# A two-block graph network on one core: where three conversions, the exponentials and the lane comparisons stand in the window stage

## The chip, the cores and the metric

The kernel runs on one core of a Trainium2 chip. The metric is the device time of the core in microseconds, from launch to end; lower is better. The engines named below are PE (matmuls), DVE (VectorE), ACT (ScalarE), POOL (GpSimd) and SP (SyncE, which issues most transfers). Each engine works through its own queue in order, and waits in it on semaphores that the others raise.

## What is computed

Two blocks over 1250 nodes with 512 features and 20000 edges, sorted by destination:

```python
h = maximum(layernorm(x), 0)
# block 0
xn   = batchnorm(h)                              # over the nodes
agg  = segment_sum(xn[src], dst) / max(deg, 1)
conv = relu(agg @ W_conv + b_conv)
attn = performer_attention(h[0:256], Wq, Wk, Wv, Wo, proj)   # 8 heads, 256 features
x = x + batchnorm(conv + attn_rows + h)
h = maximum(layernorm(x), 0)
# block 1
agg = segment_sum(h[src], dst)
z = relu(batchnorm(((1 + eps) * h + agg) @ W1 + b1))
x = x + h + relu(batchnorm(z @ W2 + b2))
```

The features of attention are `exp(u - diag - max) / 16 + 1e-6`, with the maximum over a row for queries and over a whole head for keys. `attn_rows` gives each node the attention row of its place, with node 255's row for all nodes beyond the 256th.

## The kernel before

Both segment sums are done as matmuls with a matrix of edge counts `AT` (1250 x 1250, fp16), which the kernel builds itself. The nodes are cut into 25 windows of 50 destinations. For window t, DVE writes two one-hot matrices of the window's edges: `S` (the lane of the source, one comparison for 8 chunks of 125 edges, L893) and `ring` (a code of source tile and destination, one comparison for each chunk, L897, eight to a window). PE multiplies them chunk by chunk (8 matmuls, "the counts of window t") and raises `s_win`; ACT copies the result from its bank into `AT` (L547, `AT<-bank`). From window 8 on all counts use bank 0, so the counts of window t also need ACT's copy of window t-1.

Between the counts of two windows PE does the pieces of one step, listed in `SLOTS[t]`. Step t is: PE the pieces of `SLOTS[t]`, then the counts of window t. The names that matter here:

- `hT0` to `hT9`: transposes of the normalized rows; `K`, `Q`, `V`: projections; `FR` (step 4): the sum of squares of `W_conv`, from which ACT and POOL make one scale `wscale`; `P` (step 4): small transposes.
- Attention for a pair g of heads goes through `UKg`, `MXg` (maximum over a head), `QTg`, `KVg`, `UQg`, `Og`. ACT takes the exponentials of keys in piece `MXg` (L592, L593, then L598 for the scale) and those of queries in `UQg` (L609, L610). DVE gives the biases `nbk` and `nbq` for them (L922, L929). `MXg`, `KVg` and `Og` share bank 6, so that `MX1` waits until DVE has drained `O0` (L940).
- `Gi` (steps 8 to 17, one row tile of 125 nodes each): the normalized tile times `W_conv`, as 12 fp16 matmuls over 512 columns with high and low parts (`hn_hi`, `hn_lo`, `wC_hi`, `wC_lo`). Its input comes as follows: ACT applies the batch norm (`normed(i)`, L639, four instructions into `hn`, after POOL has the scales `bn_s`, `bn_t`), DVE splits it (`normed_parts(i)`: L984 `hn_hi`, L985 `hn_lo`, which frees `hn` again), and for the weights ACT writes `wC_hi` (L649, waits for POOL's `wscale`) and DVE `wC_lo` (L1123). `hn_hi` lies where `wC` lay, so the first split waits for `wC_lo`.
- `Ri`, one step after `Gi`: PE subtracts the fp16 copy `hh` of the result (ACT's `conv_high(i)`, L547 `hh<-bank`) in the bank, and ACT reads the rest as `hl` (`conv_low(i)`). R opens with a wait for `hh`.
- `D` and `A`: degrees and the aggregation with `AT`.

What sets the order is written out by hand. ACT goes through each step as: `normed(i+2)` for a G of the step before; the pieces of the step, sorted by `late` (0 for most, 1 for `UQ` and `MX`, 2 for G, so `hh` of a step comes behind its exponentials); `conv_weights_high()` at t = `SPLIT_AT` = 5; the copy of the counts of window t. DVE goes through step t as: `low_counts(t-1)` and `further_chunks(t)`, two branches for windows or edges out of the usual bounds, neither body of which is taken for this input; `first_chunks(t+1)`, which waits for `s_win`, then writes `S` and the eight `ring`; stats of transposed tiles; `wC_lo` at t = 6; `normed_parts(t-7)`; the pieces of the step. The first and second row tile are normed on ACT at t = 6 and 7 and split on DVE at t = 7 and 8.

## Time and profile before

| | us |
|---|---|
| device time, median of 3 runs | 400.58 (400.35 to 402.19) |
| the profiled execution: device time | 401.03 |
| the profiled execution: span from first to last instruction | 399.2 |
| PE busy in the span | 363.8 |
| DVE / ACT / POOL busy | 238.6 / 174.3 / 94.5 |

The device time of the profiled execution is 1.8 us above its span; times inside are us from the span's start. The window stage takes the stretch from about 16 to 171 us, the rest is the aggregation, the second norm and block 1. A row of the timeline names start, duration, engine, line, what is written and read, and in brackets how long the engine was idle before it and who ended that. Matmuls overlap, so the distance between two starts says what one costs, not its duration.

### The profile page before, as it was taken

How to read it: one execution, taken by the hardware profiler on the slowest of the kernel's cores; microseconds unless marked ns; L12 is line 12 of the kernel's file. 1: busy time of each engine (PE TensorE's matmuls, PEld its weight loads, DVE VectorE, ACT ScalarE, POOL GpSimd, SP SyncE). 2: the span in 40 equal slices, each digit the busy share in tenths (PEclk: the TensorE clock that was granted, in tenths of full speed). 3: DMA queues.
4: the chain of work that ended last, by engine and by line, in shares of the span. 5: the costliest groups of instructions: out<-in, count | busy, mean ns of one | idle time of the engine just before them, and what ended most of it. 6: DMA issues, size and time to landing. Idle time of an engine off the chain costs nothing.

```text
span 399.2 us, 6078 instructions
## 1 busy us (share of the span) xinstructions
PE 363.8 (91%) x2031; PEld 277.5 (70%) x2031; DVE 238.6 (60%) x642; ACT 174.3 (44%) x302; POOL 94.5 (24%) x147
## 2 busy tenths in 40 slices
PE   2799983997988899999998989899999999999994
PEld 1587643675766566767655656457999999999992
DVE  5878788676576388662897788611335445421324
ACT  1446556457556513612016769312355353333031
POOL 7110101000000000000013588932265744201100
PEclk9999998799899899999999999999999999999999
DMA  6990300000000000000590020300000003020212
GB/s 187 267 253 8 106 3 2 1 2 1 3 2 3 2 2 2 2 2 2 137 226 3 1 87 21 108 2 2 0 0 2 0 2 105 0 53 13 66 51 77
DMA packets 16584, 18.03 MB, mean 45 GB/s; under 512 B 1813, under 2 KB 10965, under 8 KB 16537
## 3 DMA queue, kind: packets, MB, share of 16 engines
q1 hardware_dynamic: 15779, 17.28, 16.1%
q8 instruction: 25, 0.41, 0.4%
q10 hardware_dynamic: 758, 0.16, 0.2%
q14 instruction: 22, 0.18, 0.2%
HBM read 14.88 MB, written 2.56 MB: 44 GB/s over the span
## 4 chain that ended last, share of the span: by engine, by line
PE 68%; DVE 13%; issue 8%; ACT 4%; POOL 3%; DVEq 2%; DMA 1%; SPq 1%; POOLq 0%; ACTq 0%
PE bank L1262 65%; DVE ring L897 2%; DMA x_in<-x 1%; DVE hl L1150 1%; POOL ln_s L456 1%; DVE w_lo L1169 1%; DVE st L975 1%; POOL x L492 1%; PE bank L1283 1%; DVEq L1019 1%; DVE st_row L1161 1%; DVE hn_lo L985 1%; PE bank L1629 1%; DVE x L1158 1%; ACT hh L739 1%
## 5 line engine op out<-in xcount | busy, mean ns | idle before, releaser
L1262 PE MATMUL bank<-AT,hh 125*128 125x400 f16 (+1 forms) x240 | 81.0, 339 | 2.6 <-DVE hl L1150 2.6
L1262 PE MATMUL bank<-AT,hl 125*128 125x400 f16 (+1 forms) x240 | 80.7, 338 | 0.5 <-issue 0.5
L465 POOL TENSOR_TENSOR bn_tmp<-var_eps,minus_half 128x1 f32<-128x1 f32 (+1 forms) x15 | 9.6, 643 | 202.1 <-DVE var_eps L991 202.0
L897 DVE TENSOR_SCALAR ring<-iota_code,code 125x250 f16<-125x250 f16 x200 | 46.0, 305 | 0.0
L1262 PEld LDWEIGHTS bank<-AT,hh 125*128 125x128 f16 x240 | 23.2, 97 | 21.6 <-DVE hl L1150 3.2
L1262 PEld LDWEIGHTS bank<-AT,hl 125*128 125x128 f16 x240 | 23.4, 97 | 18.7 <-issue 1.0
L893 DVE TENSOR_TENSOR S<-iota_lane,slo 125x1024 f16<-125x1024 f16 x25 | 18.7, 748 | 29.4 <-PE bank L1262 18.4
L1262 PE MATMUL bank<-a_hi,w_hi 128*128 128x400 f32 (+1 forms) x96 | 34.2, 356 | 0.0
L1262 PE MATMUL bank<-agg_hi,w_hi 128*128 128x400 f32 (+1 forms) x96 | 34.1, 355 | 0.0
L1262 PE MATMUL bank<-a_hi,w_lo 128*128 128x400 f32 (+1 forms) x96 | 33.9, 353 | 0.0
L1262 PE MATMUL bank<-agg_hi,w_lo 128*128 128x400 f32 (+1 forms) x96 | 33.8, 352 | 0.0
L1262 PE MATMUL bank<-agg_lo,w_hi 128*128 128x400 f32 (+1 forms) x96 | 33.8, 352 | 0.0
L1262 PE MATMUL bank<-a_lo,w_hi 128*128 128x400 f32 (+1 forms) x96 | 33.8, 352 | 0.0
L1262 PE MATMUL bank<-ring,S 125*128 125x250 f16 x200 | 33.5, 310 | 0.0
L1262 PEld LDWEIGHTS bank<-ring,S 125*128 125x128 f16 x200 | 25.9, 145 | 9.9 <-issue 2.5
L970 DVE BATCH_NORM_STATS2 st_f<-zr 128x6 f32<-128x400 f32 (+1 forms) x24 | 14.2, 593 | 25.1 <-ACT zr L768 25.1
L970 DVE BATCH_NORM_STATS2 st_f<-ur 128x6 f32<-128x400 f32 (+1 forms) x12 | 6.9, 592 | 34.9 <-ACT ur L798 34.9
L768 ACT ACTIVATE zr<-bank,par 128x400 f32<-128x400 f32 (+1 forms) x24 | 14.6, 607 | 27.8 <-PE bank L1262 25.6
L520 POOL TENSOR_TENSOR a_lo<-zr,a_hi 128x1250 fp32r<-128x1250 f32 x7 | 21.2, 3025 | 16.7 <-DVE a_hi L1197 16.7
L798 ACT ACTIVATE ur<-bank,par 128x400 f32<-128x400 f32 (+1 forms) x12 | 7.2, 609 | 37.7 <-PE bank L1262 37.7
L1262 PE MATMUL bank<-wC_hi,hn_hi 128*125 128x512 f16 x40 | 17.4, 435 | 6.1 <-DVE hn_lo L985 6.1
L547 ACT ACTIVATE AT<-bank 125x500 f16<-125x500 f32 x25 | 15.1, 606 | 9.7 <-PE bank L1262 9.4
(208 smaller groups left out, 745.4 us busy)
## 6 DMA issues: line engine op xcount, KB each, us to landing
x_in<-x SPq DMA_DIRECT2D x5, 448.0 KB
x<-x SPq DMA_DIRECT2D x2, 1120.0 KB
w_s<-w SPq DMA_DIRECT2D x2, 1024.0 KB, 10.2
w_s<-w SPq DMA_DIRECT2D x4, 512.0 KB, 3.9
out<-x SPq DMA_DIRECT2D x8, 224.0 KB
wB<-wk SPq DMA_DIRECT2D x1, 1024.0 KB, 9.0
wA<-wq SPq DMA_DIRECT2D x1, 1024.0 KB, 13.5
wC<-w_conv SPq DMA_DIRECT2D x1, 1024.0 KB, 16.5
```

Source lines behind the costliest of these rows:

```text
L456: own.step(pool.tensor_tensor(s, ln_tmp[:, 0, i:i + n], minus_half[0:L, 0:n], ALU.pow))
L465: own.step(pool.tensor_tensor(bn_tmp[:, 1, k:k + n], var_eps[:, k:k + n], minus_half[:, 0:n], ALU.pow))
L492: pool.tensor_tensor(x1[:, i, :], x1[:, i, :], hring1[:, i % 3, :], ALU.add).then_inc(sem("s_x1h"), 1)
L520: pool.tensor_tensor(a_lo[:, b, :], zr[:, b % 2, :], a_hi[:, b, :].bitcast(F32), ALU.subtract)\
L547: return act.activation(o, i, ACT.Copy, scale=scale)
L739: act.activation(hh[:, i, :], x1[:, i, :], ACT.Relu, bias=ln_b[:, i:i + 1], scale=ln_s[:, i:i + 1]).then_inc(sem("s_hhb"), 1)
L768: ins = act.activation(zr[:, b % 2, c0:c0 + w], ps[:, 0:w], ACT.Identity, bias=pcol("b1", b))
L798: ins = act.activation(ur[:, f % 2, c0:c0 + w], ps[:, 0:w], ACT.Identity, bias=pcol("b2", f))
L893: dve.tensor_tensor(S[:, slot], iota_lane[0:CH], a, ALU.is_equal)
L897: return dve.tensor_scalar(ring[:, slot, j, a:b], iota_code[0:CH, a:b], code[:, bass.ds(c + j, 1)], float(-CODES * t), ALU.subtract, ALU.i ...
L970: return dve.bn_stats(st_f[:, f, ci, :], ap)
L1262: return pe.matmul(o, l, r, start=start, stop=stop, skip_group_check=True)
```

## The change

Three edits, all to the order inside the window stage:

1. **Conversions of the weights and of the first row tile.** ACT's `wC_hi` moves from the end of step 5 into piece `FR` of step 4, behind the copy of the sum of squares. DVE's `wC_lo` stays in step 6, and the split of row tile 0 (`hn_hi`, `hn_lo`) moves from step 7 to directly behind it, in front of piece `MX0`. The splits of the other tiles keep their steps.
2. **Exponentials.** On ACT the pieces `UQ` and `MX` of a step come last, behind the copy of the counts; the other pieces keep the order of `SLOTS`.
3. **Lanes.** `S` of window t+1 is written by its own function, `first_lanes(t+1)`, which now stands (with its wait for `s_win`) ahead of the two branches; the eight `ring` stay behind them.

No instruction is added or removed on any engine, and the orders of PE, POOL and SP are unchanged.

```diff
--- before.py
+++ after.py
@@ -78,7 +78,7 @@
     "G0 UK1", "KV0 UQ1 R0 G1", "O0 R1 G2", "MX1 R2 G3", "QT1 R3 G4", "KV1 UK2 R4 G5", "O1 UQ2 R5 G6", "R6 G7",
     "MX2 R7 G8", "QT2 R8 G9", "KV2 UK3 R9 D0", "O2 UQ3 A00", "A10", "MX3 A20", "QT3 A30", "KV3 D1 A01",
     "O3 A11", "TA0 TA1 A21 WO0 WO1")]
-SQ_AT, SPLIT_AT, H_AT = 2, 5, 6
+SQ_AT, SPLIT_AT, H_AT = 2, 6, 6
 
 LONE_FROM = 8
 COUNT_BANK = [t % 2 if t < LONE_FROM else 0 for t in range(NW)]
@@ -680,7 +680,7 @@
 
 
             def late(name):
-                return 2 if name[0] == "G" else name[:2] in ("UQ", "MX")
+                return name[:2] in ("UQ", "MX")
 
             for t in range(len(SLOTS)):
                 if t == H_AT:
@@ -688,12 +688,13 @@
                 for name in SLOTS[t - 1] if t else ():
                     if name[0] == "G" and int(name[1]) + 2 < T:
                         normed(int(name[1]) + 2)
-                for name in sorted(SLOTS[t], key=late) if t else ():
+                for name in [n for n in SLOTS[t] if not late(n)] if t else ():
                     if name == "FR":
                         ps = read_group(act, name)
                         copy(wcol[:, 0:1], ps[:, 0:1], 1.0 / D).then_inc(sem("s_fr"), 1)
                         act.wait_ge(sem("s_fr"), 1)
                         act.sem_inc(free[PLACE[name][0]], 1)
+                        conv_weights_high()
                     elif name[0] == "G":
                         conv_high(int(name[1]))
                     elif name[0] == "R":
@@ -707,13 +708,14 @@
                         rows(i)
                 if t == SQ_AT:
                     conv_weights()
-                if t == SPLIT_AT:
-                    conv_weights_high()
                 if t == H_AT + 1:
                     normed(1)
                 if t < NW:
                     act.wait_ge(sem("s_win"), t + 1)
                     copy(at_of(AT, t), counts_of(t)).then_inc(sem("s_at"), 1)
+                for name in SLOTS[t]:
+                    if late(name):
+                        attention(name)
 
             for f in range(FB):
                 act.wait_ge(sem("s_bn2"), f + 1)
@@ -1018,12 +1020,15 @@
             def load_range(t):
                 dve.load([lo_r[t % 2], out_r[t % 2]], win[t:t + 1, :])
 
-            def first_chunks(t):
-
-                lo = dve.snap(lo_r[t % 2], min_val=0, max_val=NCH - 1)
+            def first_lanes(t):
+
                 if t >= 2:
                     dve.wait_ge(sem("s_win"), t - 1)
-                lanes(t % 2, lo)
+                lanes(t % 2, dve.snap(lo_r[t % 2], min_val=0, max_val=NCH - 1))
+
+            def first_chunks(t):
+
+                lo = dve.snap(lo_r[t % 2], min_val=0, max_val=NCH - 1)
                 for n, j in enumerate(CHUNK_ORDER):
                     ins = one_hot(t % 2, t, lo, j, *CHUNK_COLS[j])
                     if n % Q == Q - 1:
@@ -1091,6 +1096,7 @@
                             own.mark(feature_stats(f, ci, hT[:, f, COLS[ci][0]:sum(COLS[ci])]))
 
             dve.load([lo_r[0]], ranges[0:1, 0:1])
+            first_lanes(0)
             first_chunks(0)
             row_stats(4)
             row_stats(5)
@@ -1099,6 +1105,9 @@
             load_range(0)
             load_range(1)
             for t in range(NW):
+
+                if t + 1 < NW:
+                    first_lanes(t + 1)
                 if t:
                     low_counts(t - 1)
                 further_chunks(t)
@@ -1118,11 +1127,13 @@
                                 own.mark(dve.bn_aggr(mv_f[:, f, :], st_1[:, f].rearrange("p c s -> p (c s)")))
                             own.after(own.n)
                             feature_terms(0, FB).then_inc(sem("s_mv1"), 1)
-                if t == SPLIT_AT + 1:
+                if t == SPLIT_AT:
                     dve.wait_ge(sem("s_wch"), 1)
                     dve.scalar_tensor_tensor(wC_lo[:], wC[:], wscale[:, 0:1], wC_hi[:], ALU.mult, ALU.subtract)\
                        .then_inc(sem("s_wcl"), 1)
-                if 0 <= t - H_AT - 1 < T:
+                if t == SPLIT_AT:
+                    normed_parts(0)
+                if 0 < t - H_AT - 1 < T:
                     normed_parts(t - H_AT - 1)
                 for name in SLOTS[t]:
                     piece(name)
```

ACT, steps 4 and 5, before: the four exponentials of `UQ0`, the counts of window 4, V0's copy, then `wC_hi` and the counts of window 5.

```order
L609 ACTIVATE qf<-bank,nbq 128x256
L610 ACTIVATE qf<-bank,nbq 128x256
L609 ACTIVATE qf<-bank,nbq 128x256
L610 ACTIVATE qf<-bank,nbq 128x256
L547 ACTIVATE AT<-bank 125x2x10x25
L547 ACTIVATE vaug<-bank 128x8x64
L649 ACTIVATE wC_hi<-wC,wscale 128x2048
L547 ACTIVATE AT<-bank 125x2x10x25
```

ACT, the same place in the changed kernel:

```order
L649 ACTIVATE wC_hi<-wC,wscale 128x2048
L547 ACTIVATE AT<-bank 125x2x10x25
L609 ACTIVATE qf<-bank,nbq 128x256
L610 ACTIVATE qf<-bank,nbq 128x256
L609 ACTIVATE qf<-bank,nbq 128x256
L610 ACTIVATE qf<-bank,nbq 128x256
L547 ACTIVATE vaug<-bank 128x8x64
L547 ACTIVATE AT<-bank 125x2x10x25
```

`wC_hi` and the counts now stand ahead of the exponentials and of V0's copy (`vaug`).

ACT, step 11 and the beginning of step 12, before: behind the tile norm and the low part come six instructions of `MX1` (four exponentials `kf<-bank`, two scalings), and only then `hh` of G3 and the counts of window 11.

```order
L639 ACTIVATE hn<-hT,bn_t,bn_s 128x125 x4
L547 ACTIVATE hl<-bank 125x512
L592 ACTIVATE kf<-bank,nbk 128x256
L593 ACTIVATE kf<-bank,nbk 128x256
L592 ACTIVATE kf<-bank,nbk 128x256
L593 ACTIVATE kf<-bank,nbk 128x256
L598 ACTIVATE kf<-kf,keps 128x512 x2
L547 ACTIVATE hh<-bank 125x512
L547 ACTIVATE AT<-bank 125x2x10x25
L639 ACTIVATE hn<-hT,bn_t,bn_s 128x125 x4
L625 ACTIVATE qfT<-bank,keps 128x512 x2
```

ACT, the same steps in the changed kernel:

```order
L639 ACTIVATE hn<-hT,bn_t,bn_s 128x125 x4
L547 ACTIVATE hl<-bank 125x512
L547 ACTIVATE hh<-bank 125x512
L547 ACTIVATE AT<-bank 125x2x10x25
L592 ACTIVATE kf<-bank,nbk 128x256
L593 ACTIVATE kf<-bank,nbk 128x256
L592 ACTIVATE kf<-bank,nbk 128x256
L593 ACTIVATE kf<-bank,nbk 128x256
L598 ACTIVATE kf<-kf,keps 128x512 x2
L639 ACTIVATE hn<-hT,bn_t,bn_s 128x125 x4
L625 ACTIVATE qfT<-bank,keps 128x512 x2
```

`hh` and the counts are in front, and the next tile norm (`hn`) stands directly behind the exponentials instead of behind the counts.

DVE, end of step 6 and beginning of step 7, before (the last seven rows are the two branches with the first rows of their bodies):

```order
L1031 REGISTER_ALU
L1019 TENSOR_LOAD win
L1123 SCALAR_TENSOR_TENSOR wC_lo<-wC,wscale,wC_hi 128x2048
L919 TENSOR_REDUCE kmaxall<-bank 128x2
L922 SCALAR_TENSOR_TENSOR nbk<-diag,kmaxall 128x4
L1010 COMPARE_AND_BRANCH
L1012 TENSOR_TENSOR ATlo<-bank,AT 125x2x10x25
L1010 UNCONDITIONAL_BRANCH
L1014 UNCONDITIONAL_BRANCH
L1036 COMPARE_AND_BRANCH
L1038 TENSOR_LOAD ranges
L1039 ISA
```

DVE, the same place in the changed kernel:

```order
L1036 REGISTER_ALU
L1021 TENSOR_LOAD win
L1132 SCALAR_TENSOR_TENSOR wC_lo<-wC,wscale,wC_hi 128x2048
L986 CAST hn_hi<-hn 128x500
L987 TENSOR_TENSOR hn_lo<-hn,hn_hi 128x500
L921 TENSOR_REDUCE kmaxall<-bank 128x2
L924 SCALAR_TENSOR_TENSOR nbk<-diag,kmaxall 128x4
L1027 ISA
L895 TENSOR_TENSOR S<-iota_lane,slo 125x1024
L1012 COMPARE_AND_BRANCH
L1014 TENSOR_TENSOR ATlo<-bank,AT 125x2x10x25
L1012 UNCONDITIONAL_BRANCH
```

The split of tile 0 has come in behind `wC_lo`, and `S` stands ahead of the first branch. Before, the split of tile 0 stood one whole window later, behind `S` and eight `ring`.

## Rows read from the trace of the kernel before

**Rows 1.** The page: busy time, share of the span and instructions of each engine.
```profile
PE 363.8 (91%) x2031; PEld 277.5 (70%) x2031; DVE 238.6 (60%) x642; ACT 174.3 (44%) x302; POOL 94.5 (24%) x147
```

**Rows 2.** Windows: start:end, length, busy PE, PEld, DVE, ACT, POOL, clock, DMA, GB/s.
```profile
42.00:140.00 98.00, 82.61 (x455) 56.85 (x453) 68.40 (x222) 57.28 (x124) 3.35 (x6) 0.93 0.03 10
140.00:399.20 259.20, 249.14 (x1425) 196.06 (x1423) 138.97 (x297) 97.43 (x146) 79.19 (x107) 1.00 0.14 37
```

**Rows 3.** Waits of PE from 40 to 142 us: total, times, longest.
```profile
PE bank L1262 <- ACT hh L547: 7.1, 3, 2.8
PE bank L1262 <- DVE hn_lo L985: 6.1, 1, 6.1
```

**Rows 4.** Timeline, 47 to 70 us: what leads to G0.
```profile
47.88 1.15 POOL L479 TENSOR_TENSOR wscale<-wcol,minus_half 128x1 f32<-128x1 f32 x1
...
56.26 2.00 ACT L649 ACTIVATE wC_hi<-wC,wscale 128x2048 f16<-128x2048 f32 x1
...
56.52 3.67 PE L1262 MATMUL bank<-wB,hT 128*128 128x512 f32 x8 [1.28 <-ACT vaug L547]
...
58.91 0.17 DVE L991 TENSOR_SCALAR var_eps<-mv_f 128x4 f32<-128x4 f32 x1
...
61.40 1.65 ACT L639 ACTIVATE hn<-hT,bn_t,bn_s 128x125 f32<-128x125 f32 x4 [2.66 <-POOL bn_t L468]
...
62.07 2.34 DVE L1123 SCALAR_TENSOR_TENSOR wC_lo<-wC,wscale,wC_hi 128x2048 f16<-128x2048 f32 x1
...
64.34 0.42 DVE L919 TENSOR_REDUCE kmaxall<-bank 128x2 f32<-128x256 f32 x1
...
66.00 0.69 DVE L893 TENSOR_TENSOR S<-iota_lane,slo 125x1024 f16<-125x1024 f16 x1 [0.94 <-issue]
...
66.61 1.84 DVE L897 TENSOR_SCALAR ring<-iota_code,code 125x250 f16<-125x250 f16 x8
...
68.36 0.42 DVE L984 CAST hn_hi<-hn 128x500 f16<-128x500 f32 x1
68.81 0.68 DVE L985 TENSOR_TENSOR hn_lo<-hn,hn_hi 128x500 f16<-128x500 f32 x1
...
69.55 0.69 PE L1262 MATMUL bank<-wC_hi,hn_hi 128*125 128x512 f16 x1 [6.14 <-DVE hn_lo L985]
```

**Rows 5.** Windows: G0 and G1 alone, then stretches behind PE's waits.
```profile
69.55:74.75 5.20, 5.20 (x12) 2.59 (x12) 3.59 (x11) 1.97 (x5) 0.00 (x0) 0.52 0.00 0
80.20:82.80 2.60, 2.60 (x14) 1.65 (x13) 2.53 (x9) 0.60 (x1) 0.00 (x0) 1.00 0.03 6
98.00:102.00 4.00, 4.00 (x11) 2.24 (x12) 1.18 (x3) 3.50 (x8) 0.00 (x0) 0.57 0.01 4
118.00:120.00 2.00, 0.77 (x4) 0.54 (x5) 1.45 (x5) 1.88 (x6) 0.00 (x0) 1.00 0.01 4
132.00:136.00 4.00, 4.00 (x12) 2.17 (x11) 0.00 (x0) 1.58 (x3) 0.00 (x0) 0.58 0.00 0
```

**Rows 6.** Timeline, 76 to 120 us: pieces of DVE, ACT and PE there.
```profile
75.92 1.29 DVE L913 TENSOR_REDUCE kmax<-bank 128x1 f32<-128x512 f32 x2 [2.70 <-PE bank L1262]
...
81.95 0.68 DVE L928 TENSOR_REDUCE qmax<-bank 128x2 f32<-128x512 f32 x1
...
88.96 0.49 DVE L940 TENSOR_TENSOR attn<-bank,zden 128x128 f32<-128x128 f32 x2
...
89.68 0.61 PE L1262 MATMUL bank<-ident,kmax 128*128 128x128 f32 x4
...
94.60 0.47 ACT L592 ACTIVATE kf<-bank,nbk 128x256 f32<-128x256 f32 x1 [2.12 <-DVE nbk L922]
...
97.26 0.61 ACT L547 ACTIVATE hh<-bank 125x512 f16<-125x512 f32 x1
...
116.61 0.47 ACT L609 ACTIVATE qf<-bank,nbq 128x256 f32<-128x256 f32 x1 [2.10 <-DVE nbq L929]
...
118.58 0.60 ACT L547 ACTIVATE hh<-bank 125x512 f16<-125x512 f32 x1
...
119.23 0.43 PE L1262 MATMUL bank<-hh,neg_id 125*125 125x512 f16 x1 [1.58 <-ACT hh L547]
```

More of the change, by code:

```diff
@@ L1019, in load_range @@
                 dve.load([lo_r[t % 2], out_r[t % 2]], win[t:t + 1, :])
+            def first_lanes(t):
+                if t >= 2:
+                    dve.wait_ge(sem("s_win"), t - 1)
+                lanes(t % 2, dve.snap(lo_r[t % 2], min_val=0, max_val=NCH - 1))
             def first_chunks(t):
                 lo = dve.snap(lo_r[t % 2], min_val=0, max_val=NCH - 1)
-                if t >= 2:
-                    dve.wait_ge(sem("s_win"), t - 1)
-                lanes(t % 2, lo)
                 for n, j in enumerate(CHUNK_ORDER):
```

## The prediction, made before the changed kernel ran

> **What bounds the kernel now.** I read the busy times first: PE is busy 363.8 of 399.2 us [rows 1]. The windows then say where it is not: 15.4 us of PE's idle time lie between 42 and 140 us, only 10.1 in the 259 us behind, and the mean clock is 0.93 in the first stretch against 1.00 in the second [rows 2]. So the reader is to look at the waits of PE in that stretch. Two carry it: one wait of 6.1 us for DVE's `hn_lo`, in front of G0, and three, 7.1 us in total, for ACT's `hh` [rows 3]. The longest of the three is 2.8 us and the one at 119.23 is 1.58 [rows 3, 6], so the third is 7.1 - 2.8 - 1.6 = 2.7 us. The long ones stand in front of R3 and R7, behind the exponentials of MX1 and MX2; the short one in front of R6, behind those of UQ2.
>
> Some waits cost twice. G0's 12 matmuls took 5.2 us at a granted clock of 0.52, G1's took 2.6 us at 1.00 [rows 5]: the engine had stood for 6.1 us and restarted at half speed (1.2 GHz), which cost 2.6 us. Behind R3's wait the clock was 0.57 over 4 us, behind R7's 0.58 [rows 5]: each lost 4 x 0.43 = 1.7 us. Behind the 1.58 us wait it stayed at 1.00 [rows 5].
>
> **Edit 1, weights and first tile.** Before G0 the chain runs through DVE and POOL [rows 4].
> - `wC_hi` needs `wscale`, which POOL has at 47.88 + 1.15 = 49.03. Placed in FR it runs on ACT from 49.05 to 51.05, where ACT had otherwise waited for `nbq` until 53.0. Queued behind it are the counts of window 4 (ready at 50.0, now copied by 51.6, before at 55.9) and UQ0's exponentials, whose bias comes at about 51.8. Its 2.0 us cost nothing there; without that cover they would push the exponentials and V0's copy. V0's copy, now without the 2 us, is done at about 54.7, before the preceding matmuls of MX0 end (55.0), so the 1.28 us in front of V1 [rows 4] go.
> - Chain to the tile norm: DVE's `var_eps` ends at 59.1. Edit 3 (below) takes about 1.2 us out before it, so 57.9; POOL then took 2.3 us to `bn_t`, so `hn` runs from 60.2 to 61.9.
> - DVE in step 6: `S` at 58.0, ring from 59.0 to 60.7, `wC_lo` 2.3 us to 62.95 (`wC_hi` is there by then), `hn_hi` and `hn_lo` 1.1 us to 64.1. G0 starts at 64.15 instead of 69.55: **5.4 us**. What the split leaves out is the window between: `kmaxall`, 0.94 us of branches, `S`, rings, 4.0 us from 64.34 to 68.36 [rows 4].
> - The price: `kmaxall` and `nbk` now stand behind the split, 1.1 us; against 1.4 us that DVE is ahead, MX0's exponentials move from 65.1 to 64.8. Nobody is late by that. PE, done with the counts of window 7 at 61.85, waits 2.3 us instead of 6.1. No row shows the clock behind 2.3 us; it lies between 1.58 (kept) and 2.8 (1.7 us lost). I take the second, the nearer: G0 costs 1.7 us more than at full clock, not 2.6: **0.9 us** gained, 2.6 at the other bound.
>
> **Edit 2, exponentials behind the counts.** `hh` and the counts of the step come before 2.66 us of MX work (94.60 to 97.26) or 1.97 us of UQ work (116.61 to 118.58) [rows 6].
> - R3: G3's result is there one count group before QT1; `hh` and `AT` take 0.5 us each, QT1's transposes 0.9. The wait of 2.8 us and the 1.7 us of clock behind it go: **4.5 us**. What is late next is ACT's chain: its step 11 holds hl, hh, AT, MX1 and then the tile norm (1.65 us [rows 4]), split on DVE for G5. By these durations the split is done 1.9 us before G5 is due, and the scaled keys 1.5 us before KV1.
> - R6: wait of **1.6 us** goes.
> - R7 gets a new wait. Behind the counts of window 14 ACT has AT (0.8 us after their end), UQ2 (2.0), the norm (1.6), hl and hh (1.1): 5.5 us. PE has R6, G7, the counts and MX2's matmuls: 0.3 + 2.6 + 1.2 + 0.4 = 4.5. **-1.0 us.**
> - R7's old wait, 2.7, and its clock, 1.7: MX2's exponentials no longer stand between: **4.4 us**.
> The MX3 and UQ3 steps had no wait of PE, and gain nothing.
>
> **Edit 3, lanes ahead of the branches.** Where DVE had no work in flight, `S` came 0.94 us after the instruction before it, "issue" [rows 4]: the branches. `S` itself is 0.69, and the rings start 0.61 behind its start. With `S` in flight the branches run beside it, but the rings still stand behind both: 0.15 + 0.95 us instead of 0.94 + 0.61. I take **0.45 us a step**; the bounds are 0 (branches as dear as before) and 0.8 (all hidden). Where PE is the one waited for, 0.2. In steps 3, 4 and 5 together this is the 1.2 us used above (0.25 + 0.8, step 4's gap being longer, + 0.15); from G0 to MX1 it lies on the path as follows. Behind `nbk` at 64.75, DVE has four windows of 2.9 us (3.4 before), two splits of 1.1, kmax 1.29 and two qmax with biases 1.6 [rows 6]: 81.4. Tile 3's norm then ends only at 82.1 (UQ1's exponentials from 78.4, then 1.65), its split at 83.3, and O0 is drained (0.9, its last part [rows 6]) at 84.2. Before, PE went from 69.55 to MX1 at 89.68 [rows 6] without a wait, 20.1 us; now 19.2 with the better clock, which is 83.4. So MX1 waits **-0.85 us**.
>
> The Trainium skill ("Advanced Engine Details and Errata", Control Flow Timing) gives about 108 ns for a compare-and-branch and 51 ns for a plain one. By it the two pairs would be 0.32 us a step, a third of the 0.94 in this trace. The edit could then hide 0.32 at most, and the sum would come out some 0.5 us less; I go by the trace.
>
> **The sum.** 5.4 + 0.9 - 0.85 + 4.5 + 1.6 - 1.0 + 4.4 = 15.0 us. Behind step 18 DVE and ACT wait for PE again and PE is busy 249.1 of 259.2 us [rows 2], so I let the whole of it arrive at the end. The profiled execution took 401.03, so it would take 386.0; the median of the runs is 0.45 lower, so **385.6**.
>
> **The rivals.**
> - *The branches are not hidden* (edit 3 does not do what it says, 0 a step). G0 starts at 65.6, 1.45 later than in my walk, and MX1 at 86.9, 2.6 later: a gain of 12.4, **388.2**. For it: the rings stand behind the same branches as before. Against: wherever a 0.7 us instruction ran ahead of the branches in this trace, the next came with it, without a gap of 0.94.
> - *ACT's tile loop takes the place of the waits*: exponentials, then norm, then split, then G. In step 11 ACT has 5.8 us of work and PE 4.4. If half of what edit 2 gives goes back this way, 4.8 us, the time is **390.4**. Against: over four steps ACT has about 19 us of work where PE has 23.
> - *The clock falls behind the two new short waits too*: 2 x 1.7 = 3.4 us, **389.0**. Against: it held behind 1.58 us [rows 5].
> - *Better*: 0.8 a step, MX1's wait gone, G0 at full clock (1.7 + 0.85): **383.0**.
> - *Something behind 140 us does not follow PE*, and gives the gain back: about **400**. Rows 2 speak against it.
> - *Slower*: shorter waits, but in more steps, keep the clock at 1.2 GHz through the tiles. Each G at half speed costs 2.6 us [rows 5]; before, such stretches cost 2.6 + 1.7 + 1.7 = 6.0. Without its clock terms my gain is 15.0 - 0.9 - 3.4 = 10.7. All ten tiles slow cost 26, so the end is 401.0 - 10.7 + 20 = 410.3, **409.9** by the median; it is slower than before from 16.7 / 2.6 = 6.4 slow tiles on. For it: ACT, DVE and PE now run close behind each other. Against: PE's idle time between 42 and 140 us falls from 15.4 [rows 2] to about 5 us.
>
> The Trainium skill ("TensorE: Matmul & The Clock Gate") says of the gate that the default state is throttled and activity releases it; by that alone fewer and shorter idle stretches should release it for longer, against the last rival.
>
> **How the numbers follow.** Forecast 0.53; branches 0.15; ACT's loop 0.13; clock 0.08; better 0.06; later stage 0.02; slower 0.03. The likeliest is 385.6. The range takes in the forecast with both bounds of the step cost, the branches, the clock and the better case, and all but the end of ACT's loop: 382.5 to 390.5. Faster by over 0.5% (2 us, about what a measurement of this kernel can tell from no change) 0.95, the later stage as "same" 0.02, slower 0.03.
>
> **What would show it.** In the changed kernel: G0 at about 64, with a wait of about 2.3 us and half clock for up to 4 us; no wait in front of V1; `S` without 0.9 us of "issue" before it, and rings about 1 us behind it; R3 and R6 without a wait; about 0.9 us at MX1, about 1 us at R7; D0 at about 125.4 instead of 140.4; and from there the same distances as before. I am wrong if a wait for `hn_lo` or `kf` of over 1 us shows at G5 to G9 or KV1, or if the clock is below 0.9 over 75 to 120.

## The result, and the profile after

The changed kernel took 387.73 us (median of 6 runs, 386.16 to 390.34); beside it, the kernel before took 400.47 us (6 runs, 399.97 to 402.19). The ratio is 0.967 (95% interval 0.963 to 0.971), so 13 us are gained where 15 were forecast, and the time lies 2.1 us above the forecast, inside its range.

The profiled execution took 387.95 us, span 386.2. The page, busy time, share and instructions of each engine, the line that answers to [rows 1]:

```profile
PE 360.1 (93%) x2031; PEld 276.3 (72%) x2031; DVE 239.0 (62%) x642; ACT 174.3 (45%) x302; POOL 97.1 (25%) x147
```

The windows of the same run (columns as in [rows 2]): the window stage and the rest, then the stretch of G0, and what follows it up to D0.

```profile
42.00:126.00 84.00, 78.45 (x457) 55.32 (x455) 69.51 (x224) 57.43 (x124) 5.48 (x6) 0.98 0.04 13
126.00:386.20 260.20, 249.21 (x1427) 196.03 (x1423) 138.37 (x295) 97.61 (x146) 79.28 (x107) 0.99 0.14 37
65.69:69.69 4.00, 4.00 (x11) 2.27 (x12) 3.52 (x12) 3.37 (x8) 0.00 (x0) 0.57 0.02 6
70.00:128.00 58.00, 56.59 (x352) 41.79 (x352) 45.98 (x142) 42.51 (x95) 0.00 (x0) 1.00 0.01 2
```

PE did about the same work (78.45 us against 82.61 in [rows 2]; the 4 us less are mostly matmuls that no longer run at half clock) in 84 us instead of 98. Its idle time there fell from 15.4 to 5.6 us, and the clock fell at one place only, at G0. Behind D0 nothing was won, and a little was lost.

All waits of PE from 40 to 127 us that are attributed to another engine, the view of [rows 3]: total, times, longest.

```profile
PE bank L1273 <- DVE hn_lo L987: 3.3, 1, 3.3
PE bank L1273 <- ACT hT L547: 0.8, 1, 0.8
PE bank L1273 <- ACT hh L547: 0.8, 1, 0.8
PE bank L1273 <- DVE attn L942: 0.6, 1, 0.6
```

The three waits for `hh`, 7.1 us, have become one of 0.8 (in front of R7); the 6.1 in front of G0 have become 3.3; the wait in front of V1 is gone; in front of MX1 stand 0.6 us for `attn` that were not there. The wait for `hT` (at 47.4) stands in the kernel before as well. Every wait that the prediction said would come or go did so. One number is out of line: in front of G0 stand 3.3 us, not 2.3.

The timeline shows why (start, length, engine, line, operation; in brackets the idle time before it and what ended it). These rows answer to [rows 4].

```profile
49.13 2.01 ACT L649 ACTIVATE wC_hi<-wC,wscale 128x2048 f16<-128x2048 f32 x1 [1.15 <-POOL wscale L479]
...
57.78 0.17 DVE L993 TENSOR_SCALAR var_eps<-mv_f 128x4 f32<-128x4 f32 x1
57.91 0.69 DVE L895 TENSOR_TENSOR S<-iota_lane,slo 125x1024 f16<-125x1024 f16 x1
58.03 1.65 POOL L465 TENSOR_TENSOR bn_tmp<-var_eps,minus_half 128x4 f32<-128x4 f32 x1 [8.93 <-DVE var_eps L993]
...
58.64 1.85 DVE L899 TENSOR_SCALAR ring<-iota_code,code 125x250 f16<-125x250 f16 x8
...
60.40 2.34 DVE L1132 SCALAR_TENSOR_TENSOR wC_lo<-wC,wscale,wC_hi 128x2048 f16<-128x2048 f32 x1
60.62 2.19 POOL L468 TENSOR_TENSOR bn_t<-par,bn_tmp 128x4 f32<-128x4 f32 x1
...
62.84 1.64 ACT L639 ACTIVATE hn<-hT,bn_t,bn_s 128x125 f32<-128x125 f32 x4 [6.92 <-POOL bn_t L468]
...
64.51 0.42 DVE L986 CAST hn_hi<-hn 128x500 f16<-128x500 f32 x1 [1.76 <-ACT hn L639]
...
64.96 0.68 DVE L987 TENSOR_TENSOR hn_lo<-hn,hn_hi 128x500 f16<-128x500 f32 x1
65.56 0.42 DVE L921 TENSOR_REDUCE kmaxall<-bank 128x2 f32<-128x256 f32 x1
65.69 0.66 PE L1273 MATMUL bank<-wC_hi,hn_hi 128*125 128x512 f16 x1 [3.31 <-DVE hn_lo L987]
```

The reader is to see `bn_t`: a sum of two columns, 128x4, that took 2.19 us. It began 0.2 us after `wC_lo` and ended 0.07 us after it. In the kernel before, the same four instructions of POOL are, in the timeline:

```profile
59.16 1.02 POOL L465 TENSOR_TENSOR bn_tmp<-var_eps,minus_half 128x4 f32<-128x4 f32 x1 [10.13 <-DVE var_eps L991]
60.26 0.20 POOL L466 TENSOR_TENSOR bn_s<-bn_tmp,par 128x4 f32<-128x4 f32 x1
...
60.98 0.39 POOL L468 TENSOR_TENSOR bn_t<-par,bn_tmp 128x4 f32<-128x4 f32 x1
```

There `bn_t` took 0.39 us, and `wC_lo` came only at 62.07 [rows 4], after it. L465 too is longer after (1.65 against 1.02), and it began while `S` ran. The tile norm `hn`, and with it the split, waited for `bn_t`.

### The profile page after: what moved, and what is told of

Read it like the earlier page. It is cut to its first block, busy times and chain, and to the rows that moved or that the text cites. A ratio compares the mean times of both kernels' runs of the same rounds, so it can differ in the third digit from the quotient of the medians.

```text
span 386.2 us, 6055 instructions
## 1 busy us (share of the span) xinstructions
PE 360.1 (93%) x2031; PEld 276.3 (72%) x2031; DVE 239.0 (62%) x642; ACT 174.3 (45%) x302; POOL 97.1 (25%) x147
## 4 chain that ended last, share of the span: by engine, by line
PE 71%; DVE 11%; issue 7%; ACT 4%; POOL 4%; DVEq 1%; DMA 0%; SPq 0%; POOLq 0%; ACTq 0%
PE bank L1273 68%; DVE hl L1161 1%; ACT hn L639 1%; POOL ln_s L456 1%; DVE w_lo L1180 1%; DVE st L977 1%; POOL x L492 1%; PE bank L1294 1%; DVE st_row L1172 1%; DVE ring L899 1%; PE bank L1640 1%; PE bank L1465 1%; DVE x L1169 1%; DVE st_row L847 1%; ACT hh L741 1%
## 5 line engine op out<-in xcount | busy, mean ns | idle before, releaser
L465 POOL TENSOR_TENSOR bn_tmp<-var_eps,minus_half 128x1 f32<-128x1 f32 (+1 forms) x15 | 10.3, 685 | 185.5 <-DVE var_eps L993 185.4
L639 ACT ACTIVATE hn<-hT,bn_t,bn_s 128x125 f32<-128x125 f32 x40 | 16.4, 492 | 7.3 <-POOL bn_t L468 6.9
```

Source lines behind the costliest of these rows:

```text
L465: own.step(pool.tensor_tensor(bn_tmp[:, 1, k:k + n], var_eps[:, k:k + n], minus_half[:, 0:n], ALU.pow))
L639: ins = act.activation(hn[:, i % 2, f, :], hT[:, f, i * L:(i + 1) * L], ACT.Identity, bias=bn_t[:, f:f + 1], scale=bn_s[:, f:f + 1])
```

## The experiments

All times are medians; each ratio is against the kernel before, run beside it on the same chip. Distances are read from the timeline: "counts(2) to D0" is the time from the first count matmul of window 2 to the first matmul of D0 (before 39.27 to 140.38, after 39.77 to 126.46). It leaves out that the window stage starts some tenths of a us earlier or later from run to run, and 2.7 us later in the profiled execution of `only_lanes` (counts(2) at 41.98). Where places in two runs are compared below "by the distance from counts(2)", this is taken off.

| kernel | us (lowest to highest) | ratio, interval | counts(2) to D0 |
|---|---|---|---|
| before | 400.47 (399.97 to 402.19) | 1 | 101.1 |
| after | 387.73 (386.16 to 390.34) | 0.9673, 0.9634 to 0.9712 | 86.7 |
| again (the same kernel) | 387.13 (386.27 to 388.03) | 0.9658, 0.9641 to 0.9675 | 86.4 |
| only_split (edit 1) | 400.57 (398.41 to 403.91) | 0.9994, 0.9970 to 1.0018 | 99.6 |
| only_exp (edit 2) | 392.14 (391.25 to 393.21) | 0.9783, 0.9761 to 0.9804 | 91.7 |
| only_lanes (edit 3) | 397.76 (394.84 to 399.83) | 0.9903, 0.9864 to 0.9941 | 95.6 |
| no_lanes (edits 1 and 2) | 388.21 (387.32 to 388.54) | 0.9669, 0.9653 to 0.9685 | 88.3 |
| no_lanes_again | 388.08 (387.45 to 389.03) | 0.9678, 0.9663 to 0.9694 | 88.3 |
| hold | 385.86 (385.74 to 387.19) | 0.9633, 0.9617 to 0.9650 | 85.6 |
| busy | 387.49 (386.97 to 387.86) | 0.9667, 0.9654 to 0.9680 | 85.8 |
| later | 386.46 (385.41 to 387.03) | 0.9631, 0.9617 to 0.9645 | 86.7 |
| hold_later | 384.51 (384.34 to 385.12) | 0.9592, 0.9579 to 0.9605 | 84.3 |
| all3 | 384.37 (383.65 to 385.00) | 0.9586, 0.9573 to 0.9599 | 83.6 |

`only_split`, `only_exp`, `only_lanes` and `no_lanes` were run together (before beside them: 401.02), then `again`, `no_lanes_again`, `hold` and `busy` (400.94), then the last three (401.19).

### Each edit alone, and edits 1 and 2 together

**Edit 1 alone.** The kernel before with this part of the change:

```diff
-SQ_AT, SPLIT_AT, H_AT = 2, 5, 6
+SQ_AT, SPLIT_AT, H_AT = 2, 6, 6
...
+                        conv_weights_high()
...
-                if t == SPLIT_AT:
-                    conv_weights_high()
...
-                if t == SPLIT_AT + 1:
+                if t == SPLIT_AT:
...
-                if 0 <= t - H_AT - 1 < T:
+                if t == SPLIT_AT:
+                    normed_parts(0)
+                if 0 < t - H_AT - 1 < T:
```

Expected:

> The kernel before with edit 1 alone (weights' high part in FR, tile 0 split behind the weights' low part). Theory of the prediction (the terms are waits of PE): POOL's scales come as before at 61.4, the tile norm ends at 63.0, the low part of the weights at 64.4, so G0 starts at about 65.6 instead of 69.55 (4.0 us) and at half clock for less long (0.9 us). But DVE then sets MX1 through O0, so only about 2.8 us of this are left there, and the waits for hh at R3, R6 and R7 (7.1 us in all) stand as before or longer. Time about 398 us. Rival (the gain of the full change is all in G0's start, the later waits only follow from it): the waits at R3 and R7 would shrink too and the time would be 392 or less.

It gained nothing: 0.9994. Not because G0 stayed where it was. G0 began at 66.52 and waited 2.30 us, and here the clock stayed up. From counts(2) to the counts of window 9 PE was 5.8 us ahead of the kernel before. The next steps took it back: MX1 came 50.6 us behind counts(2), where it had come 50.4 behind it before. Waits of PE for ACT's `hh` (total, times, longest, 60 to 142 us), then ACT and PE around R1, then the windows behind R1's and R7's waits:

```profile
PE bank L1263 <- ACT hh L547: 10.1, 4, 2.9
```
```profile
81.16 0.47 ACT L609 ACTIVATE qf<-bank,nbq 128x256 f32<-128x256 f32 x1 [4.34 <-issue]
...
82.54 0.47 ACT L610 ACTIVATE qf<-bank,nbq 128x256 f32<-128x256 f32 x1
...
83.12 0.60 ACT L547 ACTIVATE hh<-bank 125x512 f16<-125x512 f32 x1
...
83.77 0.69 PE L1263 MATMUL bank<-hh,neg_id 125*125 125x512 f16 x1 [2.94 <-ACT hh L547]
```
```profile
83.77:88.00 4.23, 4.23 (x10) 2.31 (x11) 3.00 (x12) 2.43 (x6) 0.00 (x0) 0.50 0.00 2
...
132.00:136.00 4.00, 3.53 (x18) 2.38 (x19) 0.61 (x3) 3.02 (x6) 0.00 (x0) 1.00 0.00 0
```

There is a fourth wait for `hh`, in front of R1: with PE earlier, it is ACT's exponentials of UQ1, which end at 83.0, that stand ahead of `hh1`. It cost 2.94 us and half clock behind it (0.50 over 4.2 us, 2.1 us). In the kernel before this wait did not show, since PE was late anyway. R3 (2.79), R6 (1.59) and R7 (2.79) stayed. The 1.5 us by which D0 is nearer in the table are the clock behind R7's wait, which this time stayed at 1.00 (second row); they do not show in the time. So edit 1 without edit 2 only moves the wait, which its expectation of 398 did not have.

**Edit 2 alone.** The kernel before with this part:

```diff
-                return 2 if name[0] == "G" else name[:2] in ("UQ", "MX")
+                return name[:2] in ("UQ", "MX")
...
-                for name in sorted(SLOTS[t], key=late) if t else ():
+                for name in [n for n in SLOTS[t] if not late(n)] if t else ():
...
+                for name in SLOTS[t]:
+                    if late(name):
+                        attention(name)
```

Expected:

> The kernel before with edit 2 alone (UQ and MX of a step behind the copy of its counts on ACT). Theory: G0 still starts at about 69.5 after a wait of 6.1 us; R3's and R6's waits go with 2.8, 1.6 and 1.7 us of clock, R7's changes from 2.7 and 1.7 of clock to about 0.8: together 9.5 us, time about 391 us. Rival (ACT's tile norms, now behind the exponentials, become the bound): waits for hn_lo at G3 to G9 appear and the time is over 395 us.

8.7 us gained, 392.1 where about 391 was expected; the sum of the prediction has 4.5 + 1.6 - 1.0 + 4.4 = 9.5 for this edit, with MX1's new wait still to come off. Waits of PE from 40 to 127 us, without those for `hT` and in front of V1:

```profile
PE bank L1265 <- DVE hn_lo L988: 6.6, 1, 6.6
...
PE bank L1265 <- ACT hh L547: 0.8, 1, 0.8
PE bank L1265 <- DVE attn L943: 0.6, 1, 0.6
```

R3 and R6 have no wait, R7 has 0.8, and MX1 has its 0.6 already here: that wait comes with edit 2 alone. Between 95 and 125 us PE was busy 29.19 of 30 us at full clock. ACT's tile loop, the second rival, did not take the gain back.

**Edit 3 alone.** The kernel before with this part:

```diff
+            def first_lanes(t):
+
                 if t >= 2:
                     dve.wait_ge(sem("s_win"), t - 1)
-                lanes(t % 2, lo)
+                lanes(t % 2, dve.snap(lo_r[t % 2], min_val=0, max_val=NCH - 1))
...
             for t in range(NW):
+
+                if t + 1 < NW:
+                    first_lanes(t + 1)
```

Expected:

> The kernel before with edit 3 alone (S ahead of the two branches). Theory: 0.4 us for each step in which DVE is waited for, steps 3 to 6, so G0 starts about 1.7 us earlier (67.9); the three waits for hh get shorter by up to 0.5 us each. Time about 398 us. Rival (the branches cost the same wherever they stand): no change, 400.5 us, with rings starting 1.5 us behind the end of the instruction before S as now.

It gained 3.9 us, with an interval of 2.4 to 5.5 (the ratio times 401.02), about as expected (398). By the distance from counts(2) G0 came 2.7 us sooner (27.6 against 30.3), where 1.7 was expected. The waits for `hh` stayed, a little shorter (2.47, 1.44 and 2.46 us), and behind the last of them the clock stayed up: 1.00 over 128 to 137. That is worth another 1.7 us of the 5.5 by which D0 is nearer; no row ties it to the edit. Here POOL's `bn_t` was held as well (62.81, 2.19 us long), and it cost nothing: G0 stood behind the rings of step 7, as before.

**Edits 1 and 2**, the changed kernel with DVE's lanes behind the branches:

```diff
             def first_chunks(t):
...
+                if t >= 2:
+                    dve.wait_ge(sem("s_win"), t - 1)
+                lanes(t % 2, lo)
...
-                if t + 1 < NW:
-                    first_lanes(t + 1)
```

Expected:

> The changed kernel without edit 3 (edits 1 and 2). By the prediction's rival for it the time is 388.2 us where the whole change was put at 385.6, so 2.6 us more than the changed kernel: about 390 by its measured 387.7. G0 at about 65.6, MX1 with a longer wait than the changed kernel's 0.6 us. If the branches cost the same wherever they stand, the time is that of the changed kernel, 387.7.

388.21 (ratio 0.9669), and 388.08 (0.9678) in a second set. Alone, edits 1 and 2 gave 0.2 and 8.7 us, together 13.3: edit 1 is worth about 4 us (3.9 by the medians, 4.6 by the ratios) only when edit 2 clears the way behind it. The expected 390 was too high: without edit 3 the time is that of the rival, or 0.9 us above it. Edit 3 on top gave 0.9 us in the second set (388.08 to 387.13, and the two intervals overlap), though it was worth 3.9 alone.

The medians probably make it look smaller than it is. Three of the nine executions without edit 3 had a mean clock of 0.999 and took 387.3 to 387.5 us; the other six had 0.989 to 0.992 and took 388.0 to 389.0. All eleven with edit 3 had 0.990 to 0.992. A mean of 0.999 over 386 us leaves 0.4 us for half clock, and G0's stretch in the two profiles without edit 3 lost 2.9 (0.56 over 6.6 us), so G0 must have run at full clock in those three. At a like clock the second set has 388.8 against 387.1, from few executions, and in the profiles D0 is 1.6 to 1.9 us nearer with edit 3. Of the 1.6 us between the profiles of `no_lanes` and `after`, 0.5 is G0's start and 1.1 a shorter stretch at half clock (5.5 us from G0 to the counts of window 8, against 6.6).

The start of G0 is where more was to be had. The timeline says where it went:

```profile
61.09 0.38 POOL L468 TENSOR_TENSOR bn_t<-par,bn_tmp 128x4 f32<-128x4 f32 x1
61.50 1.64 ACT L639 ACTIVATE hn<-hT,bn_t,bn_s 128x125 f32<-128x125 f32 x4 [5.26 <-POOL bn_t L468]
62.17 2.35 DVE L1125 SCALAR_TENSOR_TENSOR wC_lo<-wC,wscale,wC_hi 128x2048 f16<-128x2048 f32 x1
...
65.81 0.69 PE L1266 MATMUL bank<-wC_hi,hn_hi 128*125 128x512 f16 x1 [2.75 <-DVE hn_lo L987]
```

Without edit 3 `wC_lo` came 0.7 us after `bn_t` was done; `hn` began at 61.50 and G0 at 65.81. By the distance from counts(2) (39.37 here, 39.77 with edit 3) `wC_lo` begins 2.2 us earlier with edit 3 and falls on POOL's last scale; `hn` begins 0.9 us later with it than without, and G0 only 0.5 us sooner (25.9 against 26.4).

### Is POOL held by DVE's instruction?

The theory: POOL's short instruction cannot go on while DVE's `wC_lo`, which reads two operands from SBUF, is in flight, and without that G0 would start about 0.9 us sooner. The rival: `bn_t` is long for a reason of POOL's own. The test keeps everything and lets DVE wait for POOL's signal before `wC_lo`. That delays `wC_lo` a little, which by the rival only costs:

```diff
                 if t == SPLIT_AT:
                     dve.wait_ge(sem("s_wch"), 1)
+                    dve.wait_ge(sem("s_bn1"), 1)
                     dve.scalar_tensor_tensor(wC_lo[:], wC[:], wscale[:, 0:1], wC_hi[:], ALU.mult, ALU.subtract)\
```

Beside it ran the changed kernel and edits 1 and 2 once more.

> The changed kernel once more, beside no_lanes_again on the same chip, to tell what edit 3 is worth on top of the other two. By the profiles, the stretch from the counts of window 2 to D0 is 1.6 us shorter with edit 3 (86.7 against 88.3 us), but 0.7 us are lost behind D0, and the two times measured so far are the same (387.7 and 388.2). Theory: about 1 us faster than without edit 3. Rival: no difference.

> The changed kernel without edit 3, again, as the partner of the run named again. Theory: about 1 us slower than that. Rival: no difference.

> The changed kernel, with one wait more: DVE starts the low part of the weights only when POOL has both scales of the batch norm. Theory (POOL's last scale instruction took 2.19 us because it met DVE's two-input instruction and had to stand until its end; it takes 0.38 us when alone): POOL is done at about 61.1 instead of 62.8, the low part runs from 61.2 to 63.5, the tile norm ends at 62.7, the split of tile 0 at 64.6, and G0 starts 0.9 us earlier in spite of the added wait; about 0.9 us less in all, 386.8. Rival (POOL's 2.19 us is a matter of POOL itself, as fetching its instructions): the instruction stays at about 2.2 us, the low part of the weights is pushed to 62.9 to 65.2, G0 starts at 66.4 and the time is 0.7 us more.

Timeline of hold:

```profile
57.13 1.65 POOL L465 TENSOR_TENSOR bn_tmp<-var_eps,minus_half 128x4 f32<-128x4 f32 x1 [8.93 <-DVE var_eps L993]
...
59.72 0.20 POOL L468 TENSOR_TENSOR bn_t<-par,bn_tmp 128x4 f32<-128x4 f32 x1
59.96 1.64 ACT L639 ACTIVATE hn<-hT,bn_t,bn_s 128x125 f32<-128x125 f32 x4 [4.93 <-POOL bn_t L468]
60.04 2.35 DVE L1133 SCALAR_TENSOR_TENSOR wC_lo<-wC,wscale,wC_hi 128x2048 f16<-128x2048 f32 x1 [0.45 <-POOL bn_t L468]
...
63.69 0.46 PE L1274 MATMUL bank<-wC_hi,hn_hi 128*125 128x512 f16 x1 [2.19 <-DVE hn_lo L987]
```

`bn_t` took 0.20 us instead of 2.19, for a wait of 0.45 us on DVE; the norm then ran beside `wC_lo` instead of behind it, and PE waited 2.19 us at G0 instead of 3.31. G0 came 24.8 us behind counts(2) instead of 25.9. The time fell by 1.3 us, from 387.13 to 385.86 (386.8 was expected). Its interval overlaps that of `again` a little and is apart from that of `no_lanes_again` (0.9617 to 0.9650 against 0.9663 to 0.9694): with POOL's scale out of the way of `wC_lo`, edit 3 is worth 2.2 us on top of the other two (1.8 by the ratios). How much of these 2 us is the hold alone can't be said closer; that the hold is there, and what ends it, is plain from the rows: in `after`, `again` and `only_lanes` `bn_t` took 2.19 us and ended 0.06 or 0.07 behind `wC_lo`, and where `wC_lo` did not run it took 0.20 to 0.39. L465 stayed at 1.65: it still begins while `S`, also of two operands, runs. In `after` `S` had 0.57 us to go, and 0.57 and the 1.02 that L465 takes otherwise are 1.59. The Trainium skill ("SBUF — State Buffer", SBUF: two separate sides) says that the two engines share one pair of ports as an exclusive lock, which a VectorE instruction with two SBUF inputs holds for its whole length against a GpSimd instruction that reads SBUF. These traces agree, with 2.19 us beside the `wC_lo` and 0.20 without it.

### What the half clock at G0 costs

The forecast charged 1.7 us for the clock behind G0's wait. This kernel fills the wait with 15 matmuls whose result nobody reads, so that PE does not stand, and lets ACT copy V1 and AT(6) before the first tile norm:

```diff
                     i = int(name[1])
+                    if i == 0:
+                        keep_busy(15, open_group(pe, name))
                     pe.wait_ge(sem("s_hns"), i + 1)
...
-                if t == H_AT:
-                    normed(0)
...
                     copy(at_of(AT, t), counts_of(t)).then_inc(sem("s_at"), 1)
+                if t == H_AT:
+                    normed(0)
```

> The changed kernel with 15 matmuls more (450 columns, into G0's bank, overwritten by G0) in front of G0's wait; for this ACT copies V1 and the counts of window 6 ahead of the norm of tile 0, which waits for POOL anyway. Theory: PE is idle for well under 1 us before G0, the clock stays at full speed, and G0 takes 2.6 instead of 4.3 us. But MX1 waits for DVE's drain of O0, whose chain (split, kmax, qmax, exponentials, tile norm, split) does not hang on PE there, so MX1 starts no earlier and its wait grows from 0.6 to about 2.3 us: no gain, 387.7 within 0.5. Rival (PE's speed sets MX1): 1.7 us faster, 386.0.

Windows and the opening of MX1 in busy:

```profile
66.00:70.00 4.00, 4.00 (x23) 2.40 (x22) 3.52 (x13) 3.59 (x8) 0.00 (x0) 1.00 0.01 2
```
```profile
85.07 0.68 PE L1273 MATMUL bank<-ident,kmax 128*128 128x128 f32 x4 [1.46 <-DVE attn L942]
```

G0 ran at full clock: 3.8 us from its start to the counts of window 8, against 5.2 in `again`. Of these 1.4 us 0.6 reached D0, and no gain can be seen at the end (387.49 against 387.13): MX1's wait grew from 0.61 to 1.46 us. MX1 needs `attn`, which DVE writes behind the split of tile 3, and that split waits for ACT. ACT and DVE in `after`, in the timeline, up to MX1:

```profile
79.53 0.60 ACT L547 ACTIVATE AT<-bank 125x500 f16<-125x500 f32 x1 [0.57 <-PE bank L1273]
80.02 0.46 ACT L609 ACTIVATE qf<-bank,nbq 128x256 f32<-128x256 f32 x1
...
82.06 1.64 ACT L639 ACTIVATE hn<-hT,bn_t,bn_s 128x125 f32<-128x125 f32 x4 [0.20 <-ACT qf L610]
...
83.73 0.42 DVE L986 CAST hn_hi<-hn 128x500 f16<-128x500 f32 x1 [1.31 <-ACT hn L639]
...
85.18 0.49 DVE L942 TENSOR_TENSOR attn<-bank,zden 128x128 f32<-128x128 f32 x2
...
85.82 0.35 PE L1273 MATMUL bank<-ident,kmax 128*128 128x128 f32 x1 [0.61 <-DVE attn L942]
```

This is a loop from PE back to PE: the counts of window 9 release ACT's copy `AT`, then come UQ1's exponentials, the norm, the split and `attn`. From the start of the copy to the start of MX1 it took 6.29 us, 79.53 to 85.82, and the same 6.29 in `again`, `hold`, `only_exp` and `no_lanes`, whenever it began. In `busy` it took 7.13, since UQ1's exponentials waited 0.73 us for their bias from DVE:

```profile
79.27 0.47 ACT L609 ACTIVATE qf<-bank,nbq 128x256 f32<-128x256 f32 x1 [0.73 <-DVE nbq L931]
```

So DVE was next in line behind G0, and most of what the clock at G0 cost (1.4 us in `again`, 1.7 in `after`) could not be had. The expected time came, but not for the expected reason: the chain to `attn` does hang on PE, through the counts of window 9, and MX1 came 0.6 us sooner (45.2 us behind counts(2), 45.8 in `again`), as did D0.

### Taking the new waits away

If ACT's exponentials of UQ1 to UQ3 come a step later, behind the norm and the split that PE waits for, MX1's and R7's waits should go:

```diff
                 for name in SLOTS[t]:
-                    if late(name):
+                    if name[:2] == "MX" or name == "UQ0":
+                        attention(name)
+                for name in SLOTS[t - 1] if t else ():
+                    if name[:2] == "UQ" and name != "UQ0":
                         attention(name)
```

Three kernels: this alone (`later`); with DVE's added wait of `hold` (`hold_later`); and with 11 dummy matmuls before G0 and ACT's copies moved as in `busy` as well (`all3`).

> The changed kernel with the exponentials of UQ1, UQ2 and UQ3 one step later on ACT (behind the counts of the step after, so behind one more tile norm); UQ0 and all MX stay. Theory (the two waits that are left after G0 are both ends of the chain UQ exponentials, tile norm, split): MX1's wait of 0.6 us goes, because tile 3 is normed and split before, and with it O0 drained; R7's wait of 0.8 us goes, because hh of G7 no longer stands behind UQ2's exponentials. About 1.4 us less, 385.8. Rival (the work only changes places in a full ACT): other waits for hh, hn_lo or the exponentials come up at G4, G9 or QT1 and QT2 and the time stays at 387.1.

> The run named hold (DVE's low part of the weights behind POOL's scales) together with the run named later. Theory: the two gains lie at different places and add: 385.9 - 1.4 = 384.5. Rival: with G0 earlier, MX1 is again bound by DVE, and only R7's 0.8 us are gained: 385.1.

> hold_later together with 11 matmuls more in front of G0 (and ACT's copies of V1 and of the counts of window 6 ahead of tile 0's norm). Theory: G0 at full clock is worth 1.7 us up to MX1, of which DVE's chain to the drain of O0 now leaves about 0.7: 383.8. In the run named busy the same matmuls were worth nothing, because that chain set MX1. Rival: they are worth nothing here either, 384.5.

Waits of PE from 40 to 127 us in hold_later, then in all3:

```profile
PE bank L1277 <- DVE hn_lo L990: 2.2, 1, 2.2
...
PE bank L1277 <- ACT hh L547: 0.3, 1, 0.3
```
```profile
PE bank L1277 <- DVE attn L945: 1.2, 1, 1.2
...
```

Both waits went, for one of 0.3 in front of R5. `later` came out at 386.46, 0.7 us above its expectation. In its profiled execution half clock lasted longer (6.7 us from G0 to the counts of window 8, against 5.2 in `again`), so that there D0 came no sooner than in `again` (86.7 against 86.4). No row shows why it lasted longer. `hold_later` did what was expected, 384.51, 1.95 less than `later` (1.6 by the ratios): the cure for POOL and the later exponentials add up. `all3` cannot be told from it (384.37, where 383.8 was expected and the rival said 384.5): D0 comes 0.7 us sooner, and the full clock at G0 again lets MX1 wait, 1.2 us. `hold_later` is faster than the changed kernel by 2.6 to 3.2 us (0.9592 against 0.9658 and 0.9673), with two small edits.

## Why the prediction was right, and where it was off

**The bound and the mechanism: right.** The forecast was that the window stage waits, not the work behind it, and that 15.0 us of waits and half clock would go. From counts(2), D0 moved by 14.4 us; 13 reached the end.

**Edit 1: the size of the first term was off, and this is where most of the miss arose.** The prediction said "POOL then took 2.3 us to `bn_t`", as in the kernel before, and from it `hn` ready at 61.9 and G0 at 64.15. Everything else in that walk held: `wC_hi` at 49.13, no wait in front of V1, `var_eps` done at 57.95 (57.9 forecast), `wC_lo` done at 62.74 (62.95). POOL took 4.9 us, 2.6 more: 0.6 in L465, beside `S`, 0.2 in L466, and 1.8 in L468, held by `wC_lo`. `hn` ended at 64.48, and G0 began at 65.69, so the term was 3.9 us instead of 5.4 in the times of the two runs. The stage started 0.5 us later in this run (counts(2) at 39.77 against 39.27), so by the distance from counts(2) it was 4.4: G0 came after 25.9 us, where the walk has 24.9. `hold` shows the cause: without the hold on POOL G0 came after 24.8 us, what the walk had. The 2.3 us were read where `wC_lo` began only after POOL was done; edit 3 moved it beside POOL.

The wait in front of V1 went, but not by edit 1, as the walk has it: it was 1.29 us with edit 1 alone, 0.86 with edit 2 alone, 0.18 with edit 3 alone and 0.56 with edits 1 and 2. It takes all three, edit 3 most of all.

**The clock at G0: right in kind** and in size (0.57 over 4 us; from G0 to the counts of window 8 it was 5.5 us against 3.8 in `busy`, the 1.7 that was charged). But full clock was worth only 0.6 or 0.7 us at D0 and nothing that can be told at the end, as `busy` and `all3` show. That it fell behind 3.31 us in `after` and 2.19 in `hold` but not behind 2.30 in `only_split` was not foreseeable from the length of the wait.

**MX1's new wait: 0.61 instead of 0.85.** The path was right (UQ1's exponentials, tile 3's norm, its split, the drain of O0; the norm ended 18.0 us behind G0, in the walk as in the trace). What the walk did not say is what starts it: it set a time behind G0 against PE's. The runs show a loop of fixed length from the counts of window 9, of the kind that the prediction itself found at R7: the same 0.61 with G0 at 68.83 (`only_exp`) and without edit 3 (`no_lanes`). What edit 3 saved on DVE between G0 and MX1 therefore bought nothing at MX1, and DVE waited 1.31 us there for ACT's norm.

**Edit 2: right.** R3's and R6's waits are gone (2.8 and 1.6, and R3's 1.7 of clock), R7 waits 0.8 instead of 2.8 (1.0 forecast), the clock stays at 1.00 from 70 to 128. In all, 8.7 us by itself. R7's clock term rests on thinner ground: `only_split` kept full clock there behind the same 2.79 us.

**Edit 3: more than forecast in each step, spent elsewhere.** In front of G0 `S` began without the idle time of the branches, and the rings stood 0.7 to 1.0 us behind its start. Measured from the end of the instruction before `S` to the first `ring`, a step with such a gap became 0.54 to 0.67 us shorter between `no_lanes` and `after`: more than the 0.45 of the forecast, and than the 0.32 that its estimate from the times of the branches allows. `var_eps` came 1.6 us nearer to counts(2), where 1.2 was forecast. Of this POOL's hold left 0.5 us at G0, and at MX1 the rest met ACT's loop. The first rival ("branches not hidden", 388.2) has nearly the time of the run, but not its mechanism: by it the rings come as late as before, and the trace shows them early. It does describe the kernel without edit 3: 388.2 and 388.1 us, and G0 and MX1 26.4 and 47.7 us behind counts(2), where the rival has 26.3 and 47.6.

**Behind D0.** From D0 to the end of the span it was 258.8 us before and 259.7 after (259.8 in `again`, 259.6 in `hold`, 259.0 and 259.3 without edit 3). "I let the whole of it arrive at the end" was 0.9 us too kind. Nearly all of it is one gap that no other engine explains. PE, behind its branch in the aggregation of the second block, in the timeline of before, then of after:

```profile
254.99 0.36 PE L1262 MATMUL bank<-AT,hl 125*128 125x450 f16 x1 [0.52 <-issue]
```
```profile
241.93 0.36 PE L1273 MATMUL bank<-AT,hl 125*128 125x450 f16 x1 [1.36 <-issue]
```

In eleven of the thirteen traces the stretch from D0 to the end, without this gap, is 258.3 or 258.4 us (`busy` 258.1, `all3` 258.5). The gap differs between two traces of one kernel (1.36 and 1.44; 0.62 and 1.00). But it is 0.52 to 1.00 us in the five traces without edit 3 and 0.98 to 1.91 in the eight with it, so it may be a price of about half a us that edit 3 pays far behind its own place. No run was made to test this, and why a gap of PE should hang on it stays open.

The difference of 1.95 us between the forecast for the profiled execution (386.0) and its time (387.95) is thus 1.06 up to D0 (1.5 at G0, 0.5 of it a later start of the stage in this run; 0.4 back by the smaller waits) and 0.9 behind it.

**The other rivals.** ACT's loop (390.4): no; PE was busy 56.59 of 58 us from 70 to 128. Clock behind the new short waits (389.0): no, 1.00 throughout. Slower (409.9): no. A later stage that gives the gain back (400): no, it took 0.9 us. "Better" (383.0) asked for G0 at full clock and no wait at MX1. Of what was tried, `all3` came nearest, at 384.4: it had the first, still waited 1.2 us at MX1, and needed POOL out of the way.

## What to carry to other kernels

When an instruction is moved forward, look at what it will then run beside, on other engines too: a duration taken from a trace holds for the neighbours that it had there, and here a wait of 0.45 us in front of a large VectorE instruction took 2 us off an instruction of GpSimd and brought the next piece of TensorE 1.1 us forward. Two waits in series on one engine hide each other: a single edit tested alone can show nothing (0.2 us here) and be worth about 4 us once the next wait is gone, so edits of one chain are judged together. A wait that closes a loop from an engine back to itself has a length of its own, and is read from the first row of the loop, not from a race between engines. A gain in front of such a wait can end in it, as most of the clock at G0 did here. And where two traces are laid side by side, places are compared by the distance from a common event, since a whole stage can start 0.5 or even 2.7 us later in one of them.

## What was not expected of the hardware

- POOL's 128x4 sum took 0.20 us while DVE stood (hold), 0.38 beside the rings (no_lanes), and 2.19 when it began 0.2 us behind a 128x2048 VectorE instruction of two SBUF operands (after).
- TensorE's granted clock did not follow the length of the wait in front of it. Behind 2.8 us it fell in one run (before, R7: 0.58 over 4 us) and stayed in another (only_split, R7: 1.00); behind 2.3 it stayed (only_split, G0), behind 2.19 it fell (hold, G0). How long it stayed down differed as well, from 5.2 to 6.7 us for the same stretch from G0 to the next counts, where full clock takes 3.8. What else decides it was not tried. Between executions of one kernel the mean clock differed too: 0.999 in three of nine without edit 3, 0.989 to 0.992 in the others.
- A gap of TensorE behind a branch, without any other engine in it, of 0.52 to 1.91 us for the same place in the program in different kernels and runs, which makes up nearly all the difference between them from D0 to the end.
